# Graph windows and a two-way ConvLSTM scan on one core: another row order, an earlier start of the scan, fc2 and edge products exchanged, GpSimd released by VectorE's last one-hot

## The chip, the cores and the metric

One core of one Trainium2 chip runs the kernel. It has five engines with queues of their own: TensorE (PE, with its weight loads PEld), VectorE (DVE), ScalarE (ACT), GpSimd (POOL) and SyncE (SP), which here issues nearly all DMAs. The metric is device microseconds (us) of one execution, the median of several.

## The reference, cut to what matters

Two layers follow each other, on x of 16 images, 48 channels, 32 x 32.

```
layer 0 (per 8x8 window, 64 nodes, C=48, O=96, K=9)
  y     = affine(conv1x1(x, fc1))                       # 48 -> 48
  idx   = top_k(-dist(normalised nodes), 9)             # per node, in its window
  feat  = [x_i, x_j - x_i] for the 9 neighbours j
  h     = max over j of gelu(affine(feat @ ew + eb))    # 96 channels
  x1    = affine(conv1x1(h, fc2)) + x                   # 96 -> 48
layer 1 (ConvLSTM scans over the 32 rows of x1, forward and backward)
  step  : gates = conv3 over width of [x1 row, h] + b   # 4 x 48 channels
          c = sigmoid(f)*c + sigmoid(i)*tanh(g);  h = sigmoid(o)*tanh(c)
  y     = w_proj @ [h_forward, h_backward]
  out   = relu(batchnorm(y)) + x1                       # statistics over all positions
```

## The kernel before, in words

**Stages.** First fc1, the node norms and their splits into parts (to some 78 us). Then the windows stage: 32 *turns*, each for one group g of 8 windows (a strip of 8 image rows and two images, 512 nodes), till some 368 us. Then the scan stage: 32 steps with two directions d, each step one row forward and one backward, with the projection in its second half. Last the statistics, relu and the final sum.

**Every engine has a program of its own**, written out in `build` and tied to the others by semaphores (`wait_ge`, `then_inc`). Nothing reorders it: an instruction that waits holds all behind it on its engine. `turns` writes a first turn pair, a loop over most, and the last three pairs unrolled. `nth(j, b, k)` is the group k turns ahead of the present one.

**One turn g on TensorE** (its `turn`): `gather` 0, `edges_rest` and `own` of g+1, `gather` 1, `fc2` of g-1, `gather` 2, `edges` of g+2, `gather` 3, `keys` of g+4. A `gather` (L607) is 8 matmuls into one half of `pz`: one-hot columns pick the neighbours' products. `edges` (L568, L570) makes the products of nodes with edge weights, from `y_hl`, which a DMA brings from `y_d`. `own` (L592) makes the node's own product into `p_out`; `fc2` (L615) writes other partitions of the same bank and so waits for the self-gelu of g+1 that reads it.

**ScalarE**: gelu 0, `ab_low`, self-gelu of g+1, gelu 1, `x1_high` of g-2, gelu 2, `fc2_out` of g-1, gelu 3, `ab_high` of g+2. **VectorE**: the maximum over neighbours of each gelu tile (`maxima` 0 to 3, L1153), with `one_hot` halves of g+1 (L1138) and `topk` of g+3 (L1121, L1129) between them, then `self_max` (L1145), both writing `hmax`. **GpSimd**: `x1_low` of g-2 and `residual` of g-1 (L1046, L1041; "x1 operations" below), released once a turn by VectorE's last `topk` operation. **SyncE**: in a turn the `y_hl` load of g+3, the residual input, `idx` of g+3 out, x1 of g-2 out, keys of g+5 in, `idx` spread to 64 partitions (`ib`).

**fp32r heads and rests.** Values are split into a rounded head and the rest. The scan's weights `wl_raw` are loaded in 11 DMAs in turn 26, scaled on GpSimd in turns 27 and 28, and split on VectorE behind the last turn: `w_xh` (head), `wl_head`, `wl_rest` and `w_e`; four DMAs then move parts of `wl_rest` into rows of `w_xh`. x1 lies in `xh`: its rest in partitions 0 to 47, its head in 64 to 111; `load_twins` and `load_third` copy head channels into the free partitions 48 to 63, 112 to 127, and into `ht`.

**The scan.** TensorE: `x_part` (L679, x1 row with `w_xh`), `h_part` (L693, edge products of h with `w_e`; L700, `ht` with `w_xh`). ScalarE: tanh of the gates (L880, L886), copies of h (L901, L895), tanh of the cell (L890). VectorE: four cell operations (L1232, L1238, L1241, L1248) and the rest of h (L1222). In steps 26 to 29 SyncE also loads x1 rows for the end into `x1r`, in front of its `ht` thirds.

## Time and profile before

| | us |
|---|---|
| median of 3 runs | 699.86 (699.62 to 704.42) |
| the profiled execution | 700.8, span 699.0 |
| TensorE / VectorE / ScalarE / GpSimd busy | 596.8 / 545.6 / 467.0 / 121.2 |
| chain that ended last, by engine | PE 46%, ACT 17%, DVE 13%, issue 13%, DMA 6% |

Busy shares are averages over all stages. In a timeline row stand start and duration in us, the engine and line, what it writes from what, how many were merged, and in brackets the idle time in front with what ended it. A gap is worth something only where other work waits behind it.

### The profile page before, as it was taken

The numbers are of one execution on the slowest core, as the hardware profiler recorded it, in microseconds if no ns is written. First come the engines' busy times: TensorE is split into PE (matmuls) and PEld (weight loads), VectorE is DVE, ScalarE is ACT, GpSimd is POOL, SyncE is SP. The second block draws the span as 40 slices with busy tenths as digits, with TensorE's granted clock in tenths as the row PEclk, the third lists the DMA queues.
The fourth block names the chain that finished last, engine by engine and source line by source line (L and its number), as shares of the span: only waits on it lengthen the run. The fifth ranks groups of instructions, "written<-read, shape, count | busy, mean of one in ns | idle before, by whom it ended". The sixth has DMA issues, their size and how long they took to land.

```text
span 699.0 us, 12676 instructions
## 1 busy us (share of the span) xinstructions
PE 596.8 (85%) x3384; PEld 341.3 (49%) x3384; DVE 545.6 (78%) x1030; ACT 467.0 (67%) x669; POOL 121.2 (17%) x106
## 2 busy tenths in 40 slices
PE   5966799999999999996864988888888999989880
PEld 1212555555555555553532555555555555555540
DVE  2668789999999999994874777777777778777775
ACT  3722468888888888884781666666666666766565
POOL 2620102222222222233537000000000000000000
PEclk9967699999999999997996999999999999999995
DMA  9847575566556656668512211111111222147525
GB/s 224 257 133 198 158 152 130 125 133 130 129 129 129 129 129 129 129 152 166 106 26 37 50 44 46 46 46 44 47 31 31 75 71 74 53 114 153 137 59 180
DMA packets 99228, 75.61 MB, mean 108 GB/s; under 512 B 51988, under 2 KB 81174, under 8 KB 98870
## 3 DMA queue, kind: packets, MB, share of 16 engines
q1 hardware_dynamic: 98438, 71.68, 44.0%
q10 hardware_dynamic: 768, 3.67, 2.1%
q8 instruction: 10, 0.16, 0.1%
q14 instruction: 12, 0.10, 0.1%
HBM read 48.56 MB, written 22.15 MB: 101 GB/s over the span
## 4 chain that ended last, share of the span: by engine, by line
PE 46%; ACT 17%; DVE 13%; issue 13%; DMA 6%; SPq 3%; ACTq 1%; DVEq 0%
PE pz L607 14%; PE pz L700 7%; PE pz L693 6%; PE p_out L615 4%; ACT he L895 3%; ACT tgo L886 3%; DMA y_d<-y 3%; ACT gel L826 3%; PE p_edge L568 3%; PE p_keys L555 2%; PE pz L679 2%; ACT selfg L820 2%; ACT tif L880 2%; PE p_edge L570 2%; DMA y_hl<-y_d 2%
## 5 line engine op out<-in xcount | busy, mean ns | idle before, releaser
L1153 DVE TENSOR_REDUCE hmax<-gel 96x128 f32<-96x1024 f32 x128 | 154.1, 1205 | 33.3 <-ACT gel L826 32.4
L826 ACT ACTIVATE gel<-pz 96x1024 f32<-96x1024 f32 x128 | 130.7, 1023 | 58.2 <-PE pz L607 56.7
L679 PE MATMUL pz<-xh,w_xh 128*112 (+1 forms) x384 | 102.9, 404 | 7.7 <-issue 7.7
L700 PE MATMUL pz<-ht,w_xh 128*112 128x512 f32 x384 | 107.2, 415 | 2.4 <-DMA ht<-xh 2.4
L890 ACT ACTIVATE tc<-c 48x512 f32<-48x512 f32 x64 | 40.2, 627 | 68.1 <-DVE c L1241 68.1
L679 PEld LDWEIGHTS pz<-xh,w_xh 128*112 128x112 f32 x384 | 68.2, 178 | 33.2 <-issue 9.4
L700 PEld LDWEIGHTS pz<-ht,w_xh 128*112 128x112 f32 x384 | 62.3, 175 | 43.1 <-issue 23.6
L1248 DVE SCALAR_TENSOR_TENSOR h<-tgo,tc 48x512 f32<-48x512 f32 x64 | 43.9, 687 | 49.4 <-ACT tc L890 49.4
L693 PE MATMUL pz<-ht,w_e 48*112 48x512 f32 x192 | 60.5, 422 | 23.5 <-ACT he L895 23.5
L1046 POOL TENSOR_TENSOR xh<-kl,xh 48x512 f32 (+1 forms) x32 | 38.6, 1208 | 175.1 <-DVE idx L1129 90.0
L1232 DVE SCALAR_TENSOR_TENSOR cu<-tif,c 48x512 f32<-48x512 f32 x64 | 44.1, 689 | 23.5 <-ACT tif L880 21.9
L607 PE MATMUL pz<-onehot,ab_hi 64*96 64x512 f32 x256 | 61.2, 474 | 1.2 <-ACT gel L826 1.0
L693 PE MATMUL pz<-he,w_e 48*112 48x512 f32 x192 | 61.8, 428 | 0.0
L880 ACT ACTIVATE tif<-pz 112x512 f32<-112x512 f32 x64 | 38.3, 598 | 34.8 <-PE pz L700 34.0
L693 PEld LDWEIGHTS pz<-ht,w_e 48*112 48x112 f32 x192 | 28.5, 174 | 58.4 <-issue 56.0
L607 PE MATMUL pz<-ident,ab_hi 64*96 64x512 f32 x256 | 51.6, 398 | 0.0
L607 PE MATMUL pz<-ident,ab_lo 64*96 64x512 f32 x256 | 51.5, 398 | 0.0
L607 PE MATMUL pz<-onehot,ab_lo 64*96 64x512 f32 x256 | 51.4, 397 | 0.0
L1041 POOL TENSOR_TENSOR kl<-side,kr 48x512 f32<-48x512 f32 x32 | 44.5, 1390 | 24.7 <-ACT side L833 18.0
L1138 DVE TENSOR_SCALAR onehot<-ib,jcol_sb 128x1024 fp32r<-128x1024 uint16 x64 | 48.4, 757 | 0.0
L615 PE MATMUL p_out<-hmax,w_sb 96*48 96x512 f32 x64 | 34.0, 613 | 15.0 <-ACT selfg L820 9.4
L1222 DVE TENSOR_TENSOR ht<-h,ht 48x512 fp32r<-48x512 f32 x62 | 42.5, 686 | 4.7 <-ACT ht L901 4.1
(124 smaller groups left out, 1023.3 us busy)
## 6 DMA issues: line engine op xcount, KB each, us to landing
ib<-idx_d SPq DMA_DIRECT2D x64, 256.0 KB, 4.4
y_d<-y SPq DMA_DIRECT2D x32, 192.0 KB, 3.2
y_hl<-y_d SPq DMA_DIRECT2D x32, 192.0 KB, 4.3
hist_d<-h SPq DMA_DIRECT2D x62, 96.0 KB, 1.9
hp<-hist_d SPq DMA_DIRECT2D x30, 192.0 KB, 2.6
kr<-xn_d SPq DMA_DIRECT2D x32, 98.0 KB
xn_d<-x_in SPq DMA_DIRECT2D x32, 96.0 KB, 2.1
kl<-xn_d SPq DMA_DIRECT2D x32, 96.0 KB
```

The costliest lines, as they stand in the source:

```text
L607: mm = pe.matmul(pz[0:O, 2 * (t % 2) + s, :], part[rows, b, t, which], moving[rows], start=(n == 0), stop=(n == 3))
L615: pe.matmul(p_out[HALF:TOP, :], w2_sb[:, :], hmax[:, b], start=True, stop=True) \
L679: pe.matmul(pz[0:TOP, 2 * d + m, :], w_xh[:, 0, d, m, t], rhs, start=(t == 0), stop=False)
L693: pe.matmul(pz[0:TOP, 2 * d + m, :], w_e[rows, d, m, t], moving(src, rows, t), start=False, stop=False)
L700: mm = pe.matmul(pz[0:TOP, 2 * d + m, :], w_xh[:, 1, d, m, t], moving(ht, slice(0, P), t), start=False, stop=(t == TAPS - 1))
L826: act.activation(gel[:, t % 2], pz[0:O, 2 * (t % 2):2 * (t % 2) + 2, :], ACT.Gelu) \
L880: act.activation(tif[0:TOP, d], pz[0:TOP, 2 * d, :], ACT.Tanh).then_inc(S["tanh_if"], 1)
L1041: pool.tensor_tensor(kl[HALF:TOP, b], side[HALF:TOP], kr[HALF:TOP, b], ALU.add) \
L1138: dve.tensor_scalar(onehot[:, b, 2 * half:2 * half + 2], ib[:, b, 2 * half:2 * half + 2], jcol_sb[:, 0:1], None, ALU.is_equal).then_inc(S[ ...
L1153: dve.tensor_reduce(dst, gel[:, t % 2].rearrange("p w (r c k) -> p w r c k", r=WS, k=KN), AX_X, ALU.max).then_inc(S["maxed"], 1)
L1232: dve.scalar_tensor_tensor(cu[HALF:TOP, d], tif[HALF:TOP, d], 1.0, c2[HALF:TOP, d], ALU.add, ALU.mult)
L1248: dve.scalar_tensor_tensor(h2[0:C, d], tgo[HALF:TOP, d], 1.0, tc[HALF:TOP, d], ALU.add, ALU.mult) \
```

## The change

The diff has these parts.

- **Row order.** `place(g)` maps the groups' strips of 8 rows to the order 0, 3, 2, 1, so that the first 16 groups give both ends of the image. Host data are read in that order; `store_x1`, `slots` and `load_xres` use it.
- **Exchanged products.** On TensorE `edges` of g+2 stands behind gather 1 and `fc2` of g-1 behind gather 2.
- **Spread weight split.** The 11 loads are issued in turn 24, the scaling is in turns 26 and 27, and VectorE's split lies in pieces in turns 29 to 31, where it has no `topk`: three heads, two masked products that write `w_xh` (head times a column `rests` of 0 or -1, plus raw), and `w_e`. The column is filled by a memset and four tiny DMAs; the four DMAs of rests are gone.
- **Immediate scan.** Twins are copied in turns 28 and 29. TensorE starts the scan when gelu 2 of the last turn has freed its half of `pz` and both masked products are there; step 0 leaves out the six edge products of each direction (h is 0). fc2, its output and the x1 operations of the last group lie within steps 0 and 1, SyncE's constants behind step 1.
- **GpSimd** waits for `onehots` (the second half of g+1) where it waited for `topk_done` of g+3.
- **x1r.** GpSimd's memset of unused partitions is gone; one DMA more for every four rows fills them.
- One turn pair more is unrolled.

```diff
-            wl_head = a("wl_head", [P, 2, 2, TAPS, TOP], F32R)
-            wl_rest = a("wl_rest", [P, 2, 2, 2, TAPS, TOP], F32R)
+            wl_head = a("wl_head", [P, 3, 2, 2, TAPS, TOP], F32R)
         x1r = sb("x1r", [P, H // 2, B * W], F32)
         w_xh = sb("w_xh", [P, 2, 2, 2, TAPS, TOP], F32R)
...
             for b in range(2):
                 turn(0, b)
-            with engine.Fori(1, GROUPS // 2 - 3) as j:
+            with engine.Fori(1, GROUPS // 2 - 4) as j:
                 for b in range(2):
                     turn(j, b)
-            for j in range(GROUPS // 2 - 3, GROUPS // 2):
+            for j in range(GROUPS // 2 - 4, GROUPS // 2):
                 for b in range(2):
                     turn(j, b)
...
-            wr, p = g // PAIRS, g % PAIRS
+            wr, p = place(g)
             return xh[first:first + C, reg(wr * WS, 0, WS), 0:(W + 1) * B] \
                 .rearrange("c r (h n) -> c h r n", h=2)[:, :, :, reg(p * (W + 1), 1, W)]
+
+        def place(g):
+
+            return g // PAIRS * 3 % WROWS, g % PAIRS
         def by_row(t):
...
-
-            def move_scan_weights():
-
-                sp.wait_ge(S["wl_split"], 3)
-                for k, first, n in ((0, C, HALF - C), (0, TOP, P - TOP), (1, C + 1, 1), (1, TOP, P - TOP)):
-                    sp.dma_start(w_xh[first:first + n, k].bitcast(F32), wl_rest[first:first + n, k].bitcast(F32)) \
-                        .then_inc(S["wl_moved"], 16)
+                sp.wait_ge(S["rests_set"], 1)
+                for k, first, n in ((0, C, HALF - C), (0, TOP, P - TOP), (1, C + 1, HALF - C - 1), (1, TOP, P - TOP)):
+                    sp.dma_start(rests[first:first + n, k:k + 1], ones_sel[0:n, 0, 0:1],
+                                 allow_slow_non_contiguous=True).then_inc(S["rests_here"], 16)
             def load_twins(s, d, b):
...
                     .then_inc(S[f"x_third{d}"], 16)
             def turn(j, b):
-                if isinstance(j, int) and nth(j, b, 0)[0] == GROUPS - 6:
+                if isinstance(j, int) and nth(j, b, 0)[0] == GROUPS - 8:
                     load_scan_weights()
-                if isinstance(j, int) and nth(j, b, 0)[0] == GROUPS - 2:
+                if isinstance(j, int) and nth(j, b, 0)[0] in (GROUPS - 4, GROUPS - 3):
+                    d = nth(j, b, 0)[0] - (GROUPS - 4)
+                    sp.wait_ge(S["x1_hi"], 2 * PAIRS)
+                    sp.wait_ge(S["pads_set"], 9)
                     for s in range(2):
-                        load_twins(s, 0, s)
-                    sp.wait_ge(S["pads_set"], 9)
-                    load_third(0, 0)
+                        load_twins(s, d, s)
+                    load_third(0, d)
                 for k, stage in ((3, load_y), (0, load_xres), (3, store_idx), (-2, store_x1), (5, load_keys),
                                  (3, spread_idx)):
...
             turns(sp, turn)
             store_x1(GROUPS - 2, 0, GROUPS // 2 - 1)
-            move_scan_weights()
-            sp.wait_ge(S["x1_hi"], GROUPS)
-            for s in range(2):
-                load_twins(s, 1, s)
-            load_third(0, 1)
-            store_x1(GROUPS - 1, 1, GROUPS // 2 - 1)
...
                     load_h(s - 1, 1 - b)
             step(0, 0)
-            with sp.Fori(0, H // 4 - 2) as j:
+            store_x1(GROUPS - 1, 1, GROUPS // 2 - 1)
+            step(1, 1)
+            for b in range(2):
+                sp.wait_ge(S[f"x1_stored{b}"], 32 * (GROUPS // 2))
+            sp.wait_ge(S["x1_split"], GROUPS)
+            sp.dma_start(wp_sb[:], wp).then_inc(S["consts2"], 16)
+            sp.dma_start(wp_low[:], wp[C:O]).then_inc(S["consts2"], 16)
+            sp.dma_start(gb_sb[:], gb).then_inc(S["consts2"], 16)
+            sp.dma_start(comb_sb[:], comb).then_inc(S["consts2"], 16)
+            with sp.Fori(1, H // 4 - 1) as j:
                 for b in range(2):
-                    s = j * 2 + (1 + b)
+                    s = j * 2 + b
                     for d in range(2):
                         load_third(s + 1, d)
-                        load_twins(s + 2, d, 1 - b)
+                        load_twins(s + 2, d, b)
                         store_h(s, d)
-            for s in range(13, 18):
+            for s in range(14, 18):
                 step(s, s % 2)
             with sp.Fori(0, H // 4 - 4) as j:
                 for b in range(2):
                     step(j * 2 + (18 + b), b)
-            sp.wait_ge(S["x1r_pads"], 1)
+            sp.wait_ge(S["wl_split"], 3)
             with sp.Fori(0, 2) as j:
                 for b in range(2):
                     i = j * 8 + 4 * b
                     sp.dma_start(x1r[0:C, reg(i, 0, 4)], x1_d[reg(i, H // 2, 4)].rearrange("r c b w -> c r (b w)")) \
+                        .then_inc(S["x1r_loaded"], 16)
+                    sp.dma_start(x1r[C:HALF, reg(i, 0, 4)],
+                                 x1_d[reg(i, H // 2, 4), 0:HALF - C].rearrange("r c b w -> c r (b w)")) \
                         .then_inc(S["x1r_loaded"], 16)
                     for k in range(4):
...
                 on(1, edges_rest)
                 on(1, own)
                 gather(g, 1, b)
+                on(2, edges)
+                gather(g, 2, b)
                 on(-1, fc2)
-                gather(g, 2, b)
-                on(2, edges)
                 gather(g, 3, b)
                 on(4, keys)
...
                 if later(s, H // 2 + 2):
                     project(s - (H // 2 + 2), b, (s - (H // 2 + 2)) // 2)
-            pe.wait_ge(S["gelus"], 4 * GROUPS)
-            pe.wait_ge(S["wl_split"], 4)
-            pe.wait_ge(S["wl_moved"], 64)
+            pe.wait_ge(S["x1_split"], 2 * PAIRS)
             pe.wait_ge(S["zeros_set"], 2)
+            pe.wait_ge(S["wl_split"], 2)
+            pe.wait_ge(S["gelus"], 4 * GROUPS - 1)
             x_part(0, 0, 0, 0)
             h_part(0, 0)
-            pe.wait_ge(S["x1_split"], GROUPS)
+            pe.wait_ge(S["gelus"], 4 * GROUPS)
             x_part(0, 1, 0, 0)
             h_part(0, 1)
             x_part(1, 0, 1, 0)
+            fc2(GROUPS - 1, 1, GROUPS // 2 - 1)
+            pe.wait_ge(S["wl_split"], 3)
             with pe.Fori(0, H // 4 - 1) as j:
                 for b in range(2):
...
                     if more:
                         h_edge(*prev)
+                    if isinstance(s, int) and s == 0 and d == 1:
+                        fc2_out(GROUPS - 1, 1, GROUPS // 2 - 1)
                     tanh_cell(s, d)
                     if d == 0:
                         tanh_i_f(s, 1)
                     elif not isinstance(s, int) or s + 1 < H:
                         tanh_i_f(s + 1, 0)
+                    if isinstance(s, int) and s == 1 and d == 0:
+                        x1_high(GROUPS - 1, 1, GROUPS // 2 - 1)
                     if d == 0 and projects:
                         keep(s - (H // 2 + 3), 1 - b)
             tanh_i_f(0, 0)
             step(0, 0)
-            with act.Fori(0, H // 4) as j:
+            step(1, 1)
+            step(2, 0)
+            with act.Fori(1, H // 4) as j:
                 for b in range(2):
...
                     pool.tensor_scalar(ap, ap, 0.5, 1.0, ALU.mult, ALU.mult).then_inc(S["wl_scaled"], 1)
                     pool.wait_ge(S["wl_scaled"], n)
-                pool.wait_ge(S["x1_sum"], GROUPS - 5 + part)
+                pool.wait_ge(S["x1_sum"], GROUPS - 6 + part)
                 if part == 0:
                     pool.wait_ge(S["wl_loaded"], 11 * 16)
+                    pool.wait_ge(S["rests_here"], 4 * 16)
+                    pool.tensor_scalar(rests[:], rests[:], -1.0, 1.0, ALU.mult, ALU.mult).then_inc(S["rests_set"], 1)
+                    pool.wait_ge(S["rests_set"], 2)
...
                                    ALU.subtract).then_inc(S["x1_split"], 1)
             def turn(j, b):
-                if exists(nth(j, b, 3)[0]):
-                    pool.wait_ge(S["topk_done"], nth(j, b, 4)[0])
+                if exists(nth(j, b, 1)[0]):
+                    pool.wait_ge(S["onehots"], nth(j, b, 2)[0] * 2)
                 for k, stage in ((-2, x1_low), (-1, residual)):
                     if exists(nth(j, b, k)[0]):
...
                 dve.tensor_reduce(dst, gel[:, t % 2].rearrange("p w (r c k) -> p w r c k", r=WS, k=KN),
                                   AX_X, ALU.max).then_inc(S["maxed"], 1)
-            def scan_weights():
-
-                dve.wait_ge(S["wl_scaled"], 9)
-                dve.tensor_copy(w_xh[:], wl_raw[:, 0:2]).then_inc(S["wl_split"], 1)
-                dve.tensor_copy(wl_head[:], wl_raw[:, 2]).then_inc(S["wl_split"], 1)
-                dve.wait_ge(S["wl_split"], 1)
-                dve.tensor_tensor(wl_rest[:], wl_raw[:, 0:2], w_xh[:].bitcast(F32), ALU.subtract) \
-                    .then_inc(S["wl_split"], 1)
-                dve.wait_ge(S["wl_split"], 2)
-                dve.tensor_tensor(w_e[:], wl_raw[:, 2], wl_head[:].bitcast(F32), ALU.subtract).then_inc(S["wl_split"], 1)
+            def scan_weights(g, part):
+
+                def head(k):
+                    dve.tensor_copy(wl_head[:, k], wl_raw[:, k]).then_inc(S["wl_heads"], 1)
+
+                def masked(k):
+                    dve.wait_ge(S["wl_heads"], k + 1)
+                    dve.scalar_tensor_tensor(w_xh[:, k], wl_head[:, k].bitcast(F32), rests[:, k:k + 1], wl_raw[:, k],
+                                             ALU.mult, ALU.add).then_inc(S["wl_split"], 1)
+
+                if g == GROUPS - 3:
+                    if part == 0:
+                        dve.wait_ge(S["wl_scaled"], 9)
+                    head(part)
+                elif part == 0:
+                    masked(g - (GROUPS - 2))
+                elif g == GROUPS - 2:
+                    head(2)
+                else:
+                    dve.wait_ge(S["wl_heads"], 3)
+                    dve.tensor_tensor(w_e[:], wl_raw[:, 2], wl_head[:, 2].bitcast(F32), ALU.subtract) \
+                        .then_inc(S["wl_split"], 1)
             def turn(j, b):
                 now = nth(j, b, 0)
                 maxima(*now, 0)
                 on(1, one_hot, 0)
                 on(3, topk, 0)
+                if not exists(nth(j, b, 3)[0]):
+                    scan_weights(now[0], 0)
                 maxima(*now, 1)
                 on(1, one_hot, 1)
                 on(3, topk, 1)
+                if not exists(nth(j, b, 3)[0]):
+                    scan_weights(now[0], 1)
                 maxima(*now, 2)
                 maxima(*now, 3)
                 self_max(*now)
-                if not exists(nth(j, b, 1)[0]):
-                    scan_weights()
             for c in range(10):
```

TensorE, the loop's turn, before: from gather 1 to the edge products (`p_out<-hmax` is fc2, `p_edge<-we_hi,y_hl` edges).

```order
L607 MATMUL pz<-onehot,ab_hi 96x512 [waits gelus,onehots]
L607 MATMUL pz<-onehot,ab_hi 96x512
L607 MATMUL pz<-onehot,ab_lo 96x512 x2
L607 MATMUL pz<-ident,ab_hi 96x512 x2
L607 MATMUL pz<-ident,ab_lo 96x512 x2
L615 MATMUL p_out<-hmax,w_sb 48x512 [waits self_gel,self_maxed]
L607 MATMUL pz<-onehot,ab_hi 96x512 [waits gelus,onehots]
L607 MATMUL pz<-onehot,ab_hi 96x512
L607 MATMUL pz<-onehot,ab_lo 96x512 x2
L607 MATMUL pz<-ident,ab_hi 96x512 x2
L607 MATMUL pz<-ident,ab_lo 96x512 x2
L568 MATMUL p_edge<-we_hi,y_hl 128x192 [waits ab_low,y_loaded0]
```

Now the edge products come directly behind gather 1:

```order
L607 MATMUL pz<-onehot,ab_hi 96x512 [waits gelus,onehots]
L607 MATMUL pz<-onehot,ab_hi 96x512
L607 MATMUL pz<-onehot,ab_lo 96x512 x2
L607 MATMUL pz<-ident,ab_hi 96x512 x2
L607 MATMUL pz<-ident,ab_lo 96x512 x2
L568 MATMUL p_edge<-we_hi,y_hl 128x192 [waits ab_low,y_loaded0]
L570 MATMUL p_edge<-we_lo,y_hl 128x192
```

and fc2 behind gather 2, ahead of gather 3:

```order
L570 MATMUL p_edge<-we_lo,y_hl 128x192
L607 MATMUL pz<-onehot,ab_hi 96x512 [waits gelus,onehots]
L607 MATMUL pz<-onehot,ab_hi 96x512
L607 MATMUL pz<-onehot,ab_lo 96x512 x2
L607 MATMUL pz<-ident,ab_hi 96x512 x2
L607 MATMUL pz<-ident,ab_lo 96x512 x2
L615 MATMUL p_out<-hmax,w_sb 48x512 [waits self_gel,self_maxed]
L607 MATMUL pz<-onehot,ab_hi 96x512 [waits gelus,onehots]
```

The wait for `y_loaded` has moved ahead of gather 2 and fc2, the wait for `self_gel` behind it.

VectorE at the end of the windows stage, before (L1232 is the scan's first cell operation):

```order
L1145 TENSOR_TENSOR hmax<-hmax,selfg 96x512
L1153 TENSOR_REDUCE hmax<-gel 96x2x8x8 x4
L1145 TENSOR_TENSOR hmax<-hmax,selfg 96x512
L1159 CAST w_xh<-wl_raw 128x2688
L1160 CAST wl_head<-wl_raw 128x1344
L1162 TENSOR_TENSOR wl_rest<-wl_raw,w_xh 128x2688
L1165 TENSOR_TENSOR w_e<-wl_raw,wl_head 128x1344
L1232 SCALAR_TENSOR_TENSOR cu<-tif,c 48x512
```

and with the change, from the `self_max` of turn 30:

```order
L1151 TENSOR_TENSOR hmax<-hmax,selfg 96x512
L1159 TENSOR_REDUCE hmax<-gel 96x2x8x8
L1169 SCALAR_TENSOR_TENSOR w_xh<-wl_head,rests,wl_raw 128x1344
L1159 TENSOR_REDUCE hmax<-gel 96x2x8x8
L1182 TENSOR_TENSOR w_e<-wl_raw,wl_head 128x1344
L1159 TENSOR_REDUCE hmax<-gel 96x2x8x8 x2
L1151 TENSOR_TENSOR hmax<-hmax,selfg 96x512
L1252 SCALAR_TENSOR_TENSOR cu<-tif,c 48x512
```

The split has moved from between the last `self_max` and the first cell operation to places between maxima.

TensorE at the start of the scan, before:

```order
L615 MATMUL p_out<-hmax,w_sb 48x512 [waits self_gel,self_maxed]
L679 MATMUL pz<-xh,w_xh 112x512 [waits zeros_set,wl_moved,x_twin00,wl_split,gelus]
L679 MATMUL pz<-xh,w_xh 112x512 x5
L693 MATMUL pz<-ht,w_e 112x512
...
L700 MATMUL pz<-ht,w_xh 112x512 [waits x_third0]
L700 MATMUL pz<-ht,w_xh 112x512 x5
L679 MATMUL pz<-xh,w_xh 112x512 [waits x_twin10,x1_split]
```

and with the change:

```order
L678 MATMUL pz<-xh,w_xh 112x512 [waits gelus,wl_split,x_twin00,zeros_set,x1_split]
L678 MATMUL pz<-xh,w_xh 112x512 x5
L699 MATMUL pz<-ht,w_xh 112x512 [waits x_third0]
L699 MATMUL pz<-ht,w_xh 112x512 x5
L678 MATMUL pz<-xh,w_xh 112x512 [waits x_twin10,gelus]
L678 MATMUL pz<-xh,w_xh 112x512 x5
L699 MATMUL pz<-ht,w_xh 112x512 [waits x_third1]
...
L678 MATMUL pz<-xh,w_xh 112x512 [waits x_twin01,tanh_if]
...
L615 MATMUL p_out<-hmax,w_sb 48x512 [waits self_gel,self_maxed]
```

The edge products (L693) and the waits for `wl_moved` are gone, and fc2 of the last group has moved behind three x parts.

## Rows read from the trace of the kernel before

**Rows 1.** The page's first line.
```profile
span 699.0 us, 12676 instructions
```

**Rows 2.** Stretches: length, busy us (instructions) by engine, granted clock share, DMA share, GB/s.
```profile
101.71:317.20 215.49, 207.48 (x1626) 122.47 (x1626) 200.48 (x477) 181.93 (x226) 61.77 (x50) 1.00 0.62 133
322.00:331.00 9.00, 5.37 (x35) 3.98 (x37) 0.42 (x2) 1.36 (x2) 3.89 (x7) 0.60 0.70 154
```

**Rows 3.** Waits from 100 to 340 us: total, times, longest.
```profile
PE p_out L615 <- ACT selfg L820: 8.1, 26, 0.4
```

**Rows 4.** Timeline of TensorE, one turn: start, duration, what, idle before it.
```profile
213.88 1.03 PE L615 MATMUL p_out<-hmax,w_sb 96*48 96x512 f32 x2 [0.29 <-ACT selfg L820]
214.84 0.47 PE L607 MATMUL pz<-onehot,ab_hi 64*96 64x512 f32 x2
...
215.94 0.36 PE L568 MATMUL p_edge<-we_hi,y_hl 97*128 97x192 f32 x1
...
218.01 0.28 PE L551 MATMUL p_keys<-mask_r,mask_l 64*128 64x256 bf16 x1
```

**Rows 5.** Timeline of VectorE, the same turns.
```profile
212.01 0.78 DVE L1145 TENSOR_TENSOR hmax<-hmax,selfg 96x512 f32<-96x512 f32 x1
...
215.04 1.20 DVE L1153 TENSOR_REDUCE hmax<-gel 96x128 f32<-96x1024 f32 x1
216.16 0.74 DVE L1138 TENSOR_SCALAR onehot<-ib,jcol_sb 128x1024 fp32r<-128x1024 uint16 x1
...
217.49 0.22 DVE L1129 FIND_INDEX8 idx<-val,p_keys 128x8 uint16<-128x64 f32 x1
...
219.26 1.22 DVE L1153 TENSOR_REDUCE hmax<-gel 96x128 f32<-96x1024 f32 x1 [0.44 <-ACT gel L826]
220.59 0.69 DVE L1145 TENSOR_TENSOR hmax<-hmax,selfg 96x512 f32<-96x512 f32 x1
```

**Rows 6.** Timeline of GpSimd, a turn and the second scaling part.
```profile
210.97 1.28 POOL L1041 TENSOR_TENSOR kl<-side,kr 48x512 f32<-48x512 f32 x1
...
342.09 4.82 POOL L1022 TENSOR_SCALAR wl_raw<-wl_raw 48x1344 f32<-48x1344 f32 x3
```

**Rows 7.** Timeline of SyncE's DMA issues in turns 25 and 26.
```profile
300.16 0.47 SPq L290 DMA_DIRECT2D y_hl<-y_d  x1
...
309.16 4.92 SPq L388 DMA_DIRECT2D wl_raw<-wl  x11
```

**Rows 8.** Timeline of TensorE, the late edge products of turn 27.
```profile
325.63 0.53 PE L568 MATMUL p_edge<-we_hi,y_hl 97*128 97x192 f32 x1 [6.29 <-DMA y_hl<-y_d]
```

**Rows 9.** Timeline of VectorE, from turn 28 to the scan's first cell.
```profile
340.89 1.22 DVE L1153 TENSOR_REDUCE hmax<-gel 96x128 f32<-96x1024 f32 x1 [0.46 <-ACT gel L826]
342.21 1.73 DVE L1145 TENSOR_TENSOR hmax<-hmax,selfg 96x512 f32<-96x512 f32 x1
...
355.58 1.33 DVE L1138 TENSOR_SCALAR onehot<-ib,jcol_sb 128x1024 fp32r<-128x1024 uint16 x1
...
368.27 1.54 DVE L1159 CAST w_xh<-wl_raw 128x2688 fp32r<-128x2688 f32 x1
...
373.38 1.54 DVE L1165 TENSOR_TENSOR w_e<-wl_raw,wl_head 128x1344 fp32r<-128x1344 f32 x1
383.83 0.69 DVE L1232 SCALAR_TENSOR_TENSOR cu<-tif,c 48x512 f32<-48x512 f32 x1 [8.91 <-ACT tif L880]
```

**Rows 10.** Timeline of TensorE, scan step 0 and the start of step 1.
```profile
378.07 2.87 PE L679 MATMUL pz<-xh,w_xh 128*112 128x512 f32 x6 [7.73 <-issue]
...
389.62 0.46 PE L693 MATMUL pz<-ht,w_e 48*112 48x512 f32 x1 [0.45 <-ACT he L895]
```

**Rows 11.** The page's groups: busy us, mean ns, idle before them and releaser.
```profile
L700 PE MATMUL pz<-ht,w_xh 128*112 128x512 f32 x384 | 107.2, 415 | 2.4 <-DMA ht<-xh 2.4
...
L880 ACT ACTIVATE tif<-pz 112x512 f32<-112x512 f32 x64 | 38.3, 598 | 34.8 <-PE pz L700 34.0
```

**Rows 12.** The page's DMA issues: KB each, us to landing.
```profile
y_hl<-y_d SPq DMA_DIRECT2D x32, 192.0 KB, 4.3
```

46 lines of the change are left out of this document (18 added, 28 removed).

## Prediction

> **What bounds the kernel now.** The page gives the span [rows 1]. The granted-clock and busy view by stretches then shows two long stages, a windows stage and a scan stage, with a gap between. In the windows stage 25 turns take 215.49 us, 8.62 us each; VectorE is busy for 200.48 of it, 8.02 a turn, and TensorE's clock is at its upper level, 2.4 GHz [rows 2]. Neither is saturated, so I looked for what the one waits for that ends last. The waits view names it: TensorE stood 8.1 us in 26 pieces before the second layer's product (fc2, L615) until ScalarE had made the self-gelu [rows 3]. The timeline of one turn shows its order: fc2 is in front of the third gather and the edge products [rows 4], so everything behind it starts late. VectorE idles 0.44 us once in a turn [rows 5].
>
> One turn is different: SyncE issues 11 loads of scan weights in a burst, the `y_hl` load queued behind it arrives only as TensorE's edge product can start at 325.63, 6.29 us late, and the clock falls to its lower level (mean 0.60 in that stretch), so that the first edge product takes 0.53 us in place of 0.36 [rows 2, 4, 7, 8].
>
> Then the change of stages: from VectorE's fourth maximum of turn 28 at 340.89 to the first weight product of scan step 1 at 389.62 are 48.7 us [rows 9, 10]. The last piece of it is pure serial work: weight split on VectorE from 368.27, its second part by DMA, scan matmuls from 378.07 on, first cell operation at 383.83.
>
> **Exchanged products.** TensorE's second gather is now followed by edge products and the third gather, 2.1 us of work (a gather is 1.10, from 214.84 to 215.94; edges and a gather are 2.07, to 218.01) [rows 4], and only then by fc2 (0.96). The self-gelu was 0.3 us late, so this covers it. The wait is 8.1/26 = 0.31 us a turn. What is late next: VectorE has 0.44 us of slack, its last search of a turn ends at 217.71 and the keys product that waits for it starts at 218.01 [rows 4, 5], so some 0.1 us stays before that becomes the wait. I take the full 0.31 for 26 turns: **-8.1 us** (ends: 0, and 0.44 x 26 = -11.4, where VectorE would be full).
>
> **The burst.** It moves from turn 26 to turn 24, with four tiny DMAs more. `y_hl` should still arrive about 16.5 us after the first load is issued, at 309.16 before [rows 7, 8]. But edges now stand in front of a gather and of fc2, so these, 1.10 + 0.96 us, which were done before the stall, are done behind it, at the slow clock (0.53/0.36, some 1.5 times): 3.1 us. The shorter turns also reach the wait some 0.5 us earlier in their schedule; against that, the turn after the stall then runs at the high clock where it was half slow. **+3.0 us** (0 to +7).
>
> **GpSimd's release.** Its two x1 operations start behind the last one-hot and no longer behind the last search, about 0.8 us earlier. Before, the second ran from 210.97 to 212.25 and touched VectorE's `hmax` operation at 212.01 [rows 5, 6]; in a turn 0.3 us shorter it would overlap more, with the new release it does not. What lies beside it now are searches and a maximum, and maxima lay beside GpSimd already. I cost it at nothing (ends -1 and +2 us in all); its cover is the slack between the last one-hot and `hmax`. Row order adds register work on GpSimd, ScalarE and SyncE, hidden in their idle time.
>
> **Scaling of the weights on GpSimd** moves from turns 27 and 28 to 26 and 27. Its first part lay in the stall; the second collided with `hmax`, 1.73 us in place of 0.69 [rows 5, 6, 9]. Now both meet a busy VectorE: **+1.0 us** (0 to +3).
>
> **Spread split and immediate scan.** The 16 first window groups now are the image rows that both scan directions begin with, so step 0 needs only the weights, free PSUM and VectorE. With the waits on the last x1, on the DMA of the rests, and on `w_e` gone, VectorE's own queue decides. Counted from 340.89, by the spacings in [rows 5, 9]: a maximum is 1.12 us (215.04 to 216.16), or 1.33 where `hmax` waits for its completion (219.26 to 220.59); `hmax` is 0.69, a one-hot 0.74 less the same overlap of 0.08. The rest of turn 28 is 1.33 + 0.69 = 2.0. Turns 29 to 31 hold nine maxima at 1.12 (10.1), three at 1.33 (4.0), three `hmax` (2.1), four one-hots (2.6), three heads at half of the 1.54 that the double-sized cast took (2.3), and two masked products and `w_e` at 1.54 each (4.6; the masked ones have the size of `w_e`). Together 27.7 us, without a gap: end at 368.6, where the first cell operation can start, against 383.83: **-15.2 us**. TensorE is ready before that: behind the second masked product VectorE still has three maxima, `w_e` and `hmax` to do, 5.8 us, so that product ends near 362.8. The 12 matmuls of step 0, forward, take 5.7 us by the slow row at 378.07 (2.87 us for six), half of it at the fast clock, and two tanh at 0.6 follow [rows 10, 11]: the input of `cv` is there between 366.9 and 369.7, against a need at 369.3. The six edge products that step 0 no longer computes are hidden then.
>
> Off that term goes contention. Seven x1 operations of GpSimd fall into this tail, where VectorE is the path. Rows show a one-hot of 1.33 us instead of 0.74 and a `hmax` of 1.73 instead of 0.69 [rows 5, 9]; I take two of the smaller kind, and some, **+1.5 us** (0 to +6).
>
> The switch from gelu to tanh on ScalarE lay in idle time. The Trainium skill (ScalarE: Activation LUTs, "What ACT_TABLE_LOAD costs") gives 2.66 us for a switch of table sets; by that, step 0's tanh would end about when VectorE is free, and the sum would be some 0.4 us higher. No row shows such a load by itself.
>
> The last fc2, its output, residual and x1 operations slip into steps 0 and 1, in idle time of TensorE and ScalarE, but beside cell operations on VectorE: **+0.5 us** (0 to +3). GpSimd's memset of `x1r` behind the last x1 goes; nothing waited for it before the loads of step 26.
>
> **The x1r load** gets a DMA more for every four rows in steps 26 to 29. TensorE waited 2.4 us for `ht` thirds in the whole trace [rows 11], in two pieces, both in these steps, behind these loads. One issue more is 0.45 us for SyncE (4.92 for eleven, [rows 7]), and about 0.5 us of transfer: **+2.0 us** over four batches, the two that had waited in full and the others in part (0 to +5).
>
> **Sum:** -8.1 + 3.0 + 1.0 - 15.2 + 1.5 + 0.5 + 2.0 = -15.3 us. The profiled execution took 700.8 us around its span of 699.0, so it should become 685.5; against the median of 699.86 that is **684.6 us**. With the ends of the single terms the likeliest case lies between 679 and 691. About 1% (7 us) is what can be told from no change.
>
> **Rivals.**
> 1. *The turn does not shrink* (12%). VectorE's search, 0.3 us before the keys product, or the one-hots become the wait as soon as fc2 goes. For: 8.02 of 8.62 us are busy. Against: it still idles 0.44. The -8.1 falls away: 692.7.
> 2. *Contention takes the tail* (12%). VectorE's two-input operations of the tail (two masked products, `w_e`, three `hmax`) each meet a GpSimd operation and wait it out whole: six at 1.28 [rows 6] are 7.7 us in place of 1.5, which makes 690.8. For: `hmax` lost 1.04 to one scaling operation. Against: GpSimd is idle most of a turn and the pairs need not meet. The Trainium skill (SBUF — State Buffer, "Who interferes with whom") states this rule, an exclusive lock in which the later one blocks fully; the rows agree in kind, with 0.6 and 1.0 us.
> 3. *A second stall behind the burst* (8%). Behind it now come two more turns with keys loads, where one had none. If the next `y_hl` or keys are late as well, another 6.3 us and some 2 us for the slow clock: 692.9. Against: the queue had drained one turn later.
> 4. *Slower: `y_hl` is late in every turn* (5%). Edges stand 2.1 us earlier in the turn, in a turn 0.3 us shorter, and a gather now queues behind them. The load of 300.16 [rows 7] is issued 4.6 us behind a keys product (218.01 plus nine turns is 295.6), and its edges come two turns less 2.1 us behind that same product, 15.2: 10.6 us for a load that lands in 4.3 [rows 4, 12]. After the change 7.9 us are left. It decides from a landing of 7.9 us on; at 9.0 each of 25 turns loses 1.1: +27.5, which makes 712. Against: the only slow one in the trace is behind the burst.
>
> That step 0 does not start early would need the order of the program not to hold; it does hold in all engines' queues, so I leave it 1%.
>
> **How the numbers follow.** My forecast has 62%, the rivals 12, 12, 8 and 5, the rest 1. Under it, 684.6 with 679 to 691; rivals 1 to 3 end at 690 to 693, some at the border of 1%, which is 692.9. So faster 0.84, same 0.11, slower 0.05. The range reaches over rivals 1 and 2 above and, below, over burst and loads costing nothing: 678 to 693.5.
>
> **What would show it.** In the profile after: turns of about 8.3 us (fc2 to fc2) and no wait before fc2; if 8.6 stays, rival 1, and VectorE has no idle piece. A stall before the edge products of some 9 us two turns earlier, with a gather and fc2 at the slow clock behind it. VectorE without a gap from turn 29 to its first cell operation, and this about 28 us behind the fourth maximum of turn 28; durations over 1.5 us in `hmax` or the masked products are the contention. Two to four waits for `ht` thirds of 1 to 2 us near the end. The prediction is wrong if ScalarE or TensorE, not VectorE, releases step 0, or if `y_hl` waits appear in more than one turn.

## The result, and the profile after

The changed kernel takes 682.74 us (median of 4, 680.25 to 684.85) against 700.11 (699.62 to 704.42) for the kernel before on the same chip: a ratio of 0.9737, 95% interval 0.9687 to 0.9788. That is 17.4 us less. The forecast was 684.6, and the size is right. One term is given to the wrong cause, and four others are off by about 1 us each. The profiled execution took 682.53 us, 18.3 less in its span than [rows 1].

The page's first line:
```profile
span 680.7 us, 12599 instructions
```
Stretches as in [rows 2]: 22 turns, the stretch of the late edge products, and the tail.
```profile
100.37:283.15 182.78, 182.49 (x1433) 107.72 (x1431) 176.38 (x419) 160.13 (x198) 54.23 (x44) 1.00 0.56 134
294.00:312.00 18.00, 13.24 (x81) 7.93 (x81) 5.89 (x10) 7.34 (x9) 1.28 (x1) 0.68 0.66 148
332.69:360.73 28.04, 24.17 (x140) 14.41 (x141) 27.59 (x28) 21.40 (x27) 13.35 (x8) 1.00 0.27 61
```
A turn is 182.78/22 = 8.31 us, where it was 8.62 [rows 2]. TensorE is now busy in 99.8% of it: 182.49 of 182.78, against 207.48 of 215.49 before. VectorE is busy 8.02 us a turn, as before. The waits view from 95 to 320 us no longer has the row of [rows 3]:
```profile
PE p_edge L568 <- DMA y_hl<-y_d: 9.4, 1, 9.4
PEld p_keys L551 <- DVE idx L1135: 8.0, 22, 0.4
```
In this window TensorE waits once, behind the burst; the second row is a weight load that waits beside running matmuls and costs nothing. Ahead of the window, in the first turn, there is a second wait for `y_hl` that the kernel before doesn't have:
```profile
82.29 0.36 PE L568 MATMUL p_edge<-we_hi,y_hl 97*128 97x192 f32 x1 [0.75 <-DMA y_hl<-y_d]
```

VectorE in one turn, and GpSimd beside it:
```profile
193.66 1.20 DVE L1159 TENSOR_REDUCE hmax<-gel 96x128 f32<-96x1024 f32 x1
195.04 1.22 DVE L1159 TENSOR_REDUCE hmax<-gel 96x128 f32<-96x1024 f32 x1 [0.19 <-ACT gel L829]
196.37 0.69 DVE L1151 TENSOR_TENSOR hmax<-hmax,selfg 96x512 f32<-96x512 f32 x1
```
```profile
193.50 1.18 POOL L1057 TENSOR_TENSOR xh<-kl,xh 48x512 f32 x1 [5.54 <-DVE onehot L1144]
194.76 1.28 POOL L1052 TENSOR_TENSOR kl<-side,kr 48x512 f32<-48x512 f32 x1
```
GpSimd's residual (L1052) ends at 196.04, 0.33 us before `hmax` (L1151) starts. That `hmax` is the only VectorE operation of a turn with two inputs from SBUF; keep it in mind.

The burst: SyncE's queue, then TensorE (they answer to [rows 7, 8]).
```profile
281.85 6.06 SPq L392 DMA_DIRECT2D wl_raw<-wl  x11
287.95 2.18 SPq L395 DMA_DIRECT2D rests<-ones_sel  x4
290.18 0.42 SPq L294 DMA_DIRECT2D y_hl<-y_d  x1
```
```profile
298.75 0.53 PE L568 MATMUL p_edge<-we_hi,y_hl 97*128 97x192 f32 x1 [9.42 <-DMA y_hl<-y_d]
...
302.66 1.94 PE L615 MATMUL p_out<-hmax,w_sb 96*48 96x512 f32 x2
```
The edge products start 16.9 us behind the first load (forecast: 16.5), and fc2 behind them takes 1.94 us at the lower level of the clock, where it is 1.06 in other turns.

VectorE from turn 28 to the first cell operation (answers to [rows 9]), and GpSimd at its end:
```profile
331.57 2.32 DVE L1159 TENSOR_REDUCE hmax<-gel 96x128 f32<-96x1024 f32 x2
...
336.40 0.85 DVE L1165 CAST wl_head<-wl_raw 128x1344 fp32r<-128x1344 f32 x1
...
352.83 1.60 DVE L1169 SCALAR_TENSOR_TENSOR w_xh<-wl_head,rests,wl_raw 128x1344 fp32r<-128x1344 f32 x1
...
355.49 1.54 DVE L1182 TENSOR_TENSOR w_e<-wl_raw,wl_head 128x1344 fp32r<-128x1344 f32 x1
...
359.39 1.31 DVE L1151 TENSOR_TENSOR hmax<-hmax,selfg 96x512 f32<-96x512 f32 x1
360.73 0.69 DVE L1252 SCALAR_TENSOR_TENSOR cu<-tif,c 48x512 f32<-48x512 f32 x1
```
```profile
352.83 2.65 POOL L1057 TENSOR_TENSOR xh<-kl,xh 48x512 fp32r<-48x512 f32 x1 [1.70 <-ACT xh L842]
355.56 2.63 POOL L1052 TENSOR_TENSOR kl<-side,kr 48x512 f32<-48x512 f32 x1
358.94 1.21 POOL L1057 TENSOR_TENSOR xh<-kl,xh 48x512 fp32r<-48x512 f32 x1 [0.75 <-ACT xh L842]
```
The fourth maximum of turn 28 is the second of the two at 331.57, and starts 1.12 us later, at 332.69 (an operation begins 1.12 behind the maximum ahead of it). From there VectorE shows no idle piece up to `cu` at 360.73: 28.04 us, where it was 42.94 (340.89 to 383.83, [rows 9]). ScalarE's last copy of x1 and the first tanh of step 0 in the same stretch:
```profile
358.22 0.64 ACT L842 ACTIVATE xh<-kl 48x512 fp32r<-48x512 f32 x1 [1.54 <-POOL kl L1052]
358.89 0.60 ACT L881 ACTIVATE tif<-pz 112x512 f32<-112x512 f32 x1
```

TensorE near the end, the waits for thirds of `ht` (two, 2.4 us, in [rows 11]):
```profile
607.65 1.69 PE L699 MATMUL pz<-ht,w_xh 128*112 128x512 f32 x6 [2.23 <-DMA ht<-xh]
...
617.61 1.68 PE L699 MATMUL pz<-ht,w_xh 128*112 128x512 f32 x6 [0.45 <-DMA ht<-xh]
...
628.87 2.22 PE L699 MATMUL pz<-ht,w_xh 128*112 128x512 f32 x6 [1.75 <-DMA ht<-xh]
```

### The profile page after: what moved, and what is told of

Read it like the earlier page. It is cut to its first block, busy times and chain, and to the rows that moved or that the text cites. A ratio compares the mean times of both kernels' runs of the same rounds, so it can differ in the third digit from the quotient of the medians.

```text
span 680.7 us, 12599 instructions
## 1 busy us (share of the span) xinstructions
PE 589.5 (87%) x3372; PEld 338.4 (50%) x3372; DVE 543.9 (80%) x1032; ACT 467.3 (69%) x669; POOL 115.8 (17%) x107
## 4 chain that ended last, share of the span: by engine, by line
PE 51%; DVE 16%; ACT 12%; issue 9%; DMA 6%; SPq 4%; ACTq 1%; DVEq 0%
PE pz L607 16%; PE pz L699 8%; PE pz L693 7%; PE p_out L615 4%; ACT he L896 4%; DVE hmax L1159 3%; ACT tgo L887 3%; DMA y_d<-y 3%; PE p_keys L555 2%; PE p_edge L568 2%; PE pz L678 2%; PE p_edge L578 2%; ACT tif L881 2%; PE p_edge L570 2%; DVE onehot L1144 1%
## 5 line engine op out<-in xcount | busy, mean ns | idle before, releaser
L699 PE MATMUL pz<-ht,w_xh 128*112 128x512 f32 x384 | 108.8, 419 | 4.4 <-DMA ht<-xh 4.4
L693 PE MATMUL pz<-ht,w_e 48*112 48x512 f32 x186 | 58.2, 419 | 25.9 <-ACT he L896 25.9
L1057 POOL TENSOR_TENSOR xh<-kl,xh 48x512 f32 (+1 forms) x32 | 40.5, 1264 | 167.1 <-DVE onehot L1144 157.9
L693 PE MATMUL pz<-he,w_e 48*112 48x512 f32 x186 | 59.5, 426 | 0.0
L693 PEld LDWEIGHTS pz<-ht,w_e 48*112 48x112 f32 x186 | 27.3, 171 | 60.2 <-issue 57.9
L1052 POOL TENSOR_TENSOR kl<-side,kr 48x512 f32<-48x512 f32 x32 | 42.3, 1323 | 30.5 <-ACT side L836 28.3
L1261 DVE SCALAR_TENSOR_TENSOR c<-cu,cv 48x512 f32<-48x512 f32 x64 | 44.1, 690 | 2.2
```

The costliest lines, as they stand in the source:

```text
L693: pe.matmul(pz[0:TOP, 2 * d + m, :], w_e[rows, d, m, t], moving(src, rows, t), start=False, stop=False)
L699: mm = pe.matmul(pz[0:TOP, 2 * d + m, :], w_xh[:, 1, d, m, t], moving(ht, slice(0, P), t), start=False, stop=(t == TAPS - 1))
L1261: dve.scalar_tensor_tensor(c2[HALF:TOP, d], cu[HALF:TOP, d], 0.5, cv[HALF:TOP, d], ALU.mult, ALU.add) \
```

## The experiments

Each kernel is the changed one with one edit, and those with "version" in their expectation build on each other. The work up to the keys product of the first turn is nearly the same in all of them, and yet this product comes at 84.47 to 87.52 us (85.92 in the changed kernel). So two columns leave that start out: **A** is the time from this product to the first cell update `c`, **B** from there to the last `c`. "Turn" is the mean over the 23 turns from the next keys product on, waits for `y_hl` in it included. The versions whose weight loads are spread also unroll more turn pairs, 6 (loads spread) or 10 (the others). The kernel before took 699.86 to 701.50 us on the chips of these runs.

| kernel | median us | ratio to before, 95% | turn | A | B |
|---|---|---|---|---|---|
| before | 700.11 | | 8.63 | 297.68 | 290.02 |
| changed | 682.74 | 0.9687 to 0.9788 | 8.31 | 276.23 | 294.27 |
| products back | 692.34 | 0.9813 to 0.9893 | 8.62 | 285.01 | 296.09 |
| GpSimd behind the search | 691.36 | 0.9856 to 0.9916 | 8.64 | 283.66 | 294.78 |
| neither of the two | 690.46 | 0.9770 to 0.9908 | 8.64 | 285.03 | 294.10 |
| x1 first | 691.70 | 0.9790 to 0.9910 | 8.30 | 286.38 | 292.80 |
| split behind | 687.74 | 0.9762 to 0.9858 | 8.30 | 282.65 | 293.21 |
| heads on ScalarE | 683.02 | 0.9680 to 0.9781 | 8.31 | 277.26 | 297.57 |
| memset of x1r | 678.05 | 0.9631 to 0.9718 | 8.31 | 276.73 | 291.43 |
| loads spread | 673.97 | 0.9596 to 0.9652 | 8.41 | 267.31 | 294.80 |
| single loads, memset | 668.56 | 0.9492 to 0.9625 | 8.32 | 263.98 | 292.77 |
| + scaling behind hmax | 669.81 | 0.9485 to 0.9602 | 8.36 | 264.82 | 293.86 |
| + heads on GpSimd | 667.80 | 0.9474 to 0.9594 | 8.34 | 263.78 | 291.91 |
| + load behind y_hl | 666.21 | 0.9454 to 0.9541 | 8.27 | 262.06 | 291.61 |

### Which edit shortened the turn

**Products back**, and **GpSimd behind the search**:
```diff
-                on(2, edges)
-                gather(g, 2, b)
                 on(-1, fc2)
+                gather(g, 2, b)
+                on(2, edges)
                 gather(g, 3, b)
```
```diff
-                if exists(nth(j, b, 1)[0]):
+                if exists(nth(j, b, 3)[0]):
+                    pool.wait_ge(S["topk_done"], nth(j, b, 4)[0])
+                elif exists(nth(j, b, 1)[0]):
                     pool.wait_ge(S["onehots"], nth(j, b, 2)[0] * 2)
```


> The changed kernel with one part undone: on TensorE the fc2 product of the group before last and the edge products of the group after next stand again in the order of before (fc2 ahead, edge products behind). Theory (the exchange is worth 0.3 us a turn): between two fc2 products 8.62 us again in place of 8.31, 22 turns and the two of the start, so about 7.4 to 8 us longer up to the burst of weight loads; at the burst fc2 no longer stands behind an edge product that waits for the residual, which gives 1 to 3 back. Total 688 to 690 us against 682.7. Rival (the 0.3 us a turn came from the earlier release of GpSimd or from another wait that the new order of x1_low and the residual took off, not from the exchange): the turn stays at 8.31, total 680 to 683.

> The changed kernel with one part undone: GpSimd waits again for the end of the whole search of VectorE in a turn, not for the last one-hot of the turn, before it makes x1_low and the residual. Theory (the release is worth nothing, since the residual is done long before the edge products that read it): turn 8.31 as in the changed kernel, total 682.7 within -1 to +2. Rival (the release carries part of the 0.3 us a turn, since the residual now lies beside the GELU product's maximum and the edge products wait for it): 0.3 to 0.7 us a turn more, 28 turns, total 690 to 700, and a wait of TensorE for GpSimd ahead of the edge products that the changed kernel does not have.

Each edit taken back alone gives the whole 0.3 us back: 8.62 and 8.64. For the first that is what the theory said (its 692.3 us are 2 above the theory's total, since B is 1.8 longer, in the last five steps where loads wait), for the second it is the rival's size (691.4 us, not 682.7), but with the wait in another place: not TensorE for GpSimd, but VectorE's own operation becomes longer. Then both together (the two edits above in one kernel):

> The changed kernel with both the order of the products and the release of GpSimd as before. Each of them undone alone gave turns of 8.63 and 8.65 us in place of 8.31. Theory (two bounds lie one behind the other, TensorE's wait for the self-gelu and VectorE's hmax behind the residual of GpSimd, and each edit takes off one, so that only both pay): turns of 8.62 to 8.66, total 689 to 692, no slower than either alone. Rival (the two are independent costs of 0.3 us each that add up): turns of 8.95, total near 700.

8.64 again, 690.46 us: the rival (8.95) is out. The costs are not added but stand one behind the other. The waits views from 100 to 280 us, first of the kernel with the products back, then of the one with GpSimd behind the search:
```profile
PE p_out L615 <- ACT selfg L823: 6.6, 21, 0.4
```
```profile
PEld p_keys L551 <- DVE idx L1137: 14.2, 21, 0.9
ACT gel L829 <- DVE hmax L1161: 8.3, 10, 0.9
```
and the turn of that second kernel on VectorE and GpSimd:
```profile
197.29 2.32 DVE L1161 TENSOR_REDUCE hmax<-gel 96x128 f32<-96x1024 f32 x2
199.71 1.32 DVE L1153 TENSOR_TENSOR hmax<-hmax,selfg 96x512 f32<-96x512 f32 x1
200.96 1.20 DVE L1161 TENSOR_REDUCE hmax<-gel 96x128 f32<-96x1024 f32 x1
```
```profile
197.95 1.19 POOL L1057 TENSOR_TENSOR xh<-kl,xh 48x512 f32 x1 [6.04 <-DVE idx L1137]
199.21 1.27 POOL L1052 TENSOR_TENSOR kl<-side,kr 48x512 f32<-48x512 f32 x1
```
The residual is still running when `hmax` is due, and `hmax` takes 1.32 in place of 0.69 us. Over 21 turns (grouped by line, three kernels: GpSimd behind the search, neither, changed):
```profile
L1153 DVE TENSOR_TENSOR hmax<-hmax,selfg 96x512 f32<-96x512 f32 x21 | 28.8, 1373 | 2.3
```
```profile
L1153 DVE TENSOR_TENSOR hmax<-hmax,selfg 96x512 f32<-96x512 f32 x21 | 21.2, 1009 | 2.3
```
```profile
L1151 DVE TENSOR_TENSOR hmax<-hmax,selfg 96x512 f32<-96x512 f32 x22 | 15.1, 689 | 2.4
```
VectorE's 8.02 us of a turn and 1.37 - 0.69 = 0.68 more are 8.70, a little over its turn of 8.64: VectorE is full. The stretches view of that kernel has it busy for 177.61 of 180 us:
```profile
100.00:280.00 180.00, 174.83 (x1357) 102.17 (x1356) 177.61 (x394) 152.68 (x188) 51.93 (x42) 1.00 0.55 129
```
In the kernel with neither edit the overlap is there too (1.01), but VectorE still has slack, and TensorE's wait for the self-gelu is back (7.0 us in 21 pieces): it sets 8.64.

### The tail

**x1 first** moves fc2, its output and x1 of the last group ahead of step 0 on TensorE and ScalarE, with a wait for all x1; **split behind** takes VectorE's split out of the turns:
```diff
             turns(pe, turn)
+            fc2(GROUPS - 1, 1, GROUPS // 2 - 1)
+            pe.wait_ge(S["x1_hi"], GROUPS)
```
```diff
             turns(dve, turn)
+            scan_weights()
```


> The changed kernel with the immediate start of the scan undone and the rest kept: TensorE and ScalarE finish fc2, its output and x1 of the last group before step 0, and step 0 waits for the last x1. Theory: fc2 1.0, its output 0.8, residual 1.3, x1_high 0.6, step 0's products 4.2 and tanh 0.6 all stand behind VectorE's last maximum, about 8.5 us in all, and the 1.3 us that the late fc2 costs in steps 0 to 2 come back: first cell operation 36 to 37 us behind the fourth maximum of turn 28 (28.0 in the changed kernel), total 689.5 to 690.5. Rival (step 0 was released by the split of the weights and not by the row order, so that the last x1 lies beside it): 1 to 3 us, total 683 to 685.5.

> The changed kernel with the split of the scan's weights (three heads, two masked products, w_e: 6.9 us on VectorE) in one piece behind the last turn, in place of one or two of its operations in each of the turns 29 to 31. Theory (spreading pays only by letting TensorE and ScalarE do step 0 beside VectorE's last operations; VectorE's own sum is the same): turns end 6.9 us earlier on VectorE, the second masked product 4.6 us behind that, step 0's products and tanh 4.7 us behind that, so the first cell operation comes 30 to 31 us behind the fourth maximum of turn 28, where it is 28.0; total 684.5 to 686. Rival (in the turns the split lies in VectorE's idle time, so that putting it behind costs all of it): 34.9 us, total 689.6.

From the fourth maximum of turn 28 to the first cell operation the changed kernel has 28.04 us. The columns of VectorE's timeline, x1 first and then split behind:
```profile
361.10 1.25 DVE L1150 TENSOR_TENSOR hmax<-hmax,selfg 96x512 f32<-96x512 f32 x1
372.05 0.69 DVE L1251 SCALAR_TENSOR_TENSOR cu<-tif,c 48x512 f32<-48x512 f32 x1 [9.71 <-ACT tif L884]
```
```profile
341.58 1.22 DVE L1159 TENSOR_REDUCE hmax<-gel 96x128 f32<-96x1024 f32 x1 [0.87 <-ACT gel L829]
...
367.88 0.69 DVE L1245 SCALAR_TENSOR_TENSOR cu<-tif,c 48x512 f32<-48x512 f32 x1 [2.67 <-ACT tif L881]
```
Their fourth maxima start at 334.41 and 333.74. So x1 first has 37.64, 9.6 us more, of which 1.2 come back in steps 0 to 2 (B is 1.47 shorter): the theory, 0.6 us above its range; the rival's 1 to 3 us are out. The excess is mostly TensorE's clock behind its wait for `hmax` (0.52 from 358 to 372 us): fc2 took 1.94 us where the theory had 1.0. Step 0's products were at the lower clock too (2.90 us for the first six, 1.66 in the changed kernel), but from their start at 367.21 to the tanh at 371.43 they took the 4.2 us of the theory.
```profile
362.40 1.94 PE L615 MATMUL p_out<-hmax,w_sb 96*48 96x512 f32 x2 [6.32 <-DVE hmax L1150]
```
Split behind has 34.14, 6.1 us more, near its rival's 34.9, and 687.74 us lies between the two forecasts. Both had a part: VectorE idled 2.4 us in turns 29 to 31, waiting for gelus (0.87 of it above), which the split had filled; and behind the second masked product stood step 0's products and tanh, at the lower clock, with 4.8 us, the theory's 4.7. The two parts, 9.6 + 6.1 = 15.7, are near what the tail gained (14.9); that they add up isn't shown, since each was undone with the other in place.

**Heads on ScalarE**:
```diff
+                def head(k):
+                    act.wait_ge(S["wl_scaled"], 9)
+                    act.activation(wl_head[:, k], wl_raw[:, k], ACT.Copy).then_inc(S["wl_heads"], 1)
...
-                def head(k):
-                    dve.tensor_copy(wl_head[:, k], wl_raw[:, k]).then_inc(S["wl_heads"], 1)
```


> The changed kernel with the three head casts of the scan's weights (0.77 us each on VectorE) moved to ScalarE, in turns 29 and 30; VectorE keeps the two masked products and w_e. Theory (VectorE's own queue is the path from turn 28 to the first cell operation): that operation comes 28.0 - 2.3 = 25.7 us behind the fourth maximum of turn 28, total 680.4 against 682.7. Rival (TensorE, released by the last GELU products and the second masked product, is as late as VectorE): the tanh of step 0 ends 0.4 us before VectorE is free in the changed kernel, so the first cell operation moves by 0.4 to 1 us alone, and waits for ScalarE's tif; total 681.7 to 682.3.

Neither: the tail became longer, 29.18 us. ScalarE and then VectorE:
```profile
345.56 1.33 ACT L851 ACTIVATE wl_head<-wl_raw 128x1344 fp32r<-128x1344 f32 x1
```
```profile
337.99 1.22 DVE L1170 TENSOR_REDUCE hmax<-gel 96x128 f32<-96x1024 f32 x1 [0.98 <-ACT gel L829]
...
339.84 1.22 DVE L1170 TENSOR_REDUCE hmax<-gel 96x128 f32<-96x1024 f32 x1 [0.63 <-ACT gel L829]
```
A head costs ScalarE 1.33 us, VectorE 0.77 (a row of 0.85, but the next operation starts 0.08 before its end). VectorE saves 2.3 and waits 3.1 for gelus in turns 29 and 30, where ScalarE is now busy for 18.68 of 19.55 us (15.21 of 18.40 in the changed kernel). VectorE is full in the changed kernel's tail, but ScalarE has too little room there for three more operations ahead of its gelus.

### The end, and the burst

**Memset of x1r**: the extra DMA for each four rows goes, and GpSimd's memset is back.
```diff
-                    sp.dma_start(x1r[C:HALF, reg(i, 0, 4)],
-                                 x1_d[reg(i, H // 2, 4), 0:HALF - C].rearrange("r c b w -> c r (b w)")) \
-                        .then_inc(S["x1r_loaded"], 16)
...
+            pool.memset(x1r[32:HALF], 0.0).then_inc(S["x1r_pads"], 1)
```


> The changed kernel without the extra transfer for rows 48 to 63 of the reversed copy of x1: those rows are set to zero once by GpSimd behind the last x1, as in the kernel before, and no output depends on them. Theory (that transfer, one more in each of the eight loads of the last steps on SyncE's queue, makes the last rows of the scan late): cells from (27,0) to the end come 2.5 to 3 us earlier, total 679.5 to 680.5 against 682.7. Rival (the late rows hang on the row transfers as a whole, and the one more is nothing): less than 0.5 us, total 682.3 to 682.7.

B is 291.43, 2.84 us shorter: the theory holds. The median is 4.7 less, where the theory had 2.2 to 3.2; the rest lies in the other stages, in the profiled executions 1.4 of it in the start. The changed kernel and the seven others with the extra DMA differ by up to 2.1 us among each other from step 25 to step 31, but all four later versions without it are, with this one, 1.8 to 2.9 us shorter there than the changed kernel. The three waits of TensorE for `ht` are 2.13 in all, where they were 4.43 (two of the three):
```profile
605.70 1.67 PE L696 MATMUL pz<-ht,w_xh 128*112 128x512 f32 x6 [1.07 <-DMA ht<-xh]
...
625.76 1.68 PE L696 MATMUL pz<-ht,w_xh 128*112 128x512 f32 x6 [0.73 <-DMA ht<-xh]
```

**Loads spread** over six turns, then **single loads** over eleven:
```diff
-                if isinstance(j, int) and nth(j, b, 0)[0] == GROUPS - 8:
-                    load_scan_weights()
...
+                if isinstance(j, int) and GROUPS - 12 <= nth(j, b, 0)[0] < GROUPS - 6:
+                    load_scan_weights(nth(j, b, 0)[0] - (GROUPS - 12))
```


> The changed kernel with the eleven loads of the scan's weights and the four of the rests no longer issued in one go at turn 24 on SyncE's queue, but one to three at a time behind the other work of turns 20 to 25. Theory (the burst delays the y_hl loads that the edge products read by one whole wait, 9.42 us of idle TensorE, and what follows at the lower clock): the wait is gone, total 9 to 11 us less, 672 to 674. Rival (the transfers themselves, not their issue in one go, take the time, or the turn after has no room for the scaling): half of it or less, total 677 to 682.

> A version from the experiments: the changed kernel with rows 48 to 63 of x1's reversed copy set to zero once by GpSimd in place of the extra transfer, and the eleven loads of the scan's weights one to a turn in turns 12 to 22, the four of the rests in turn 23. Theory (spread over six turns the loads still left waits of TensorE for y_hl of 2.7 us in all, from two or three loads in one turn; one to a turn leaves none): 2 to 3 us below the sum of the two single experiments (682.7 - 8.8 - 4.7 = 669.2), so 666 to 668. Rival (one large load in a turn delays the y_hl behind it as much as two do): 668.5 to 671, with y_hl waits in several turns.

Spread, the median is 8.8 us less and A 8.9, 673.97 in all: the theory. The waits left (2.7 us) are mostly one:
```profile
282.82 0.36 PE L571 MATMUL p_edge<-we_hi,y_hl 97*128 97x192 f32 x1 [2.11 <-DMA y_hl<-y_d]
```
Single loads leave one of 0.6, and A is 3.3 shorter still. By A that is the theory. The median, 668.56, is just in the rival's range and only 0.6 below the sum of the two single experiments (B gave back 1.3), but what the rival named, waits in several turns, isn't there.

### What the experiments point to

> The version with single loads, and the scaling of the weights by GpSimd cut into three parts in turns 24 to 26 in place of two in turns 26 and 27, each behind VectorE's hmax of its turn. Theory (in the changed kernel the scaling holds hmax up once, 1.68 in place of 0.69 us, and one-hots by 0.2, so behind hmax it costs nothing): 0.8 to 1.5 us less than the version with single loads, no hmax over 0.8 us in turns 24 to 28. Rival (the scaling then meets one-hots and maxima and costs as much there): within 0.3 us of it.

> The version with scaling behind hmax, and the three head casts moved from VectorE to GpSimd, in turns 27 and 28 behind hmax. Theory (VectorE and ScalarE share the tail: without any part of the split VectorE still waited 2.4 us for ScalarE's gelus in turns 29 to 31, so of the 2.3 us of heads about half lies in such waits): first cell operation 1 to 1.5 us earlier against the fourth maximum of turn 28, total 1 to 1.5 us less. Rival (ScalarE is the path of the tail as soon as the heads go, as in the version with the heads on ScalarE): less than 0.4 us.

> The version with the heads on GpSimd, and each single load of the scan's weights issued right behind the y_hl load of its turn in place of right ahead of the next turn's y_hl. Theory (the waits for y_hl that were left, 1.5 us in two pieces, come from the largest loads standing directly ahead of y_hl in SyncE's queue): no wait for y_hl before TensorE's edge products in turns 12 to 28, 1 to 1.5 us less than before, total 666 to 667. Rival (the weight loads take the time of the DMA engines wherever they stand, and delay the keys or the gathers' indices instead): no gain, total 667.5 to 669.

```diff
+                pool.wait_ge(S["self_maxed"], GROUPS - 8 + part + 1)
...
+                for k in ((0, 1) if g == GROUPS - 5 else (2,)):
+                    pool.tensor_copy(wl_head[:, k], wl_raw[:, k]).then_inc(S["wl_heads"], 1)
...
+                    if stage is load_y and isinstance(j, int) and GROUPS - 20 <= nth(j, b, 0)[0] < GROUPS - 8:
+                        load_scan_weights(nth(j, b, 0)[0] - (GROUPS - 20))
```
Scaling behind `hmax`: the operation itself is cured, as the timelines show (single loads, then this one), but the time is 1.2 longer and not 0.8 to 1.5 shorter (669.81 against 668.56, intervals overlap):
```profile
311.86 1.69 DVE L1153 TENSOR_TENSOR hmax<-hmax,selfg 96x512 f32<-96x512 f32 x1
```
```profile
313.87 0.69 DVE L1155 TENSOR_TENSOR hmax<-hmax,selfg 96x512 f32<-96x512 f32 x1
```
Its trace has 1.8 us of `y_hl` waits where that of single loads has 0.6, with the same queue; from the last keys product on it is 0.3 us shorter. Neither theory nor rival, and inconclusive. Heads on GpSimd: the first cell operation comes 27.12 us behind the fourth maximum of turn 28, against 28.12, which is the theory's 1 us; but 0.4 of that is lost ahead of this maximum, and from the last keys product to the first `c` it is 38.33 us against 38.97, so 0.6. With the load moved behind `y_hl` the waits for it from turn 2 on fall from 1.5 us to none and A by 1.7: the theory. This version takes **666.21 us**, 0.9498 of before (0.9454 to 0.9541), below both kernels of this case.

## Why the prediction was right, and where it was not

By its own terms, from the two profiles:

| term | forecast | measured |
|---|---|---|
| start, same code | 0 | -1.65 |
| products and release, 26 turns | -8.1 + 0 | -9.5 |
| burst, scaling | +3.0 + 1.0 | +2.9 |
| tail: split, immediate scan, contention | -15.2 + 1.5 | -14.9 |
| last x1 in steps 0 to 2 | +0.5 | +1.3 |
| x1r load, and the last stretch | +2.0 | +2.95 + 0.55 |
| sum | -15.3 | -18.3 |

How the second column is read: the keys product of the first turn comes at 85.92 against 87.57, that of the next turn gains 1.46 more, the next 23 gain 7.40, and two further turns count 0.62. The fourth maximum of turn 28 comes 8.20 earlier (332.69, 340.89), so 9.5 + 1.65 - 8.2 = 2.9 went to burst and scaling. `cu` is 23.1 earlier, the updates from step 2 on 21.8, the last 18.85. The 1.65 of the start belong to no edit: this product comes anywhere from 84.47 to 87.52 in the kernels of the table above, whose work up to there is nearly the same. That they are part of the 18.3 is chance.

- **Exchanged products: the size is right, the step that names its cause failed.** The size is even nearer than the table says. A turn gains 0.32 us, 8.3 in 26 turns. The other 1.1 lie in one turn, where the kernel before waited 1.30 us for a search and then ran at the lower clock (mean 0.83 from 85 to 95 us; 1.00 in the changed kernel). "I cost it at nothing", of GpSimd's release, was half of the pair: with the exchange alone the turn is 8.64, with the release alone 8.62, with neither 8.64, with both 8.31. The prediction had the mechanism in a sentence (a shorter turn lets the residual overlap `hmax` more, the release prevents it) and gave it no price. Whoever had made only the exchange on that sum would have got nothing. It was readable: VectorE busy for 8.02 us has 0.29 of slack in a turn of 8.31, and an `hmax` held up by half of the residual's 1.28 [rows 6] uses up more. Rival 1 was this case, with the wrong operation as the full engine's load.
- **The burst.** One stall, two turns earlier, with a gather and fc2 at the lower clock: as told. With the exchange taken back the three turns around the stall took 37.34 us, 11.5 over three of its own turns; in the changed kernel 37.63, 12.7 over. So the new order costs 1.2 us at the stall, and 3.0 was too much: with the products back the turn behind the stall took 11.51 us, in the changed kernel 8.32. Rival 3 did not come.
- **The tail.** 28.04 us against 27.7 and 1.5 of contention. The contention fell on the other side: while VectorE was first (the masked product at 352.83, `w_e` at 355.49) GpSimd took 2.65 and 2.63 in place of 1.2 and 1.28, and VectorE's own time was 1.60 and 1.54, as without it. VectorE lost 0.62 once, at the `hmax` of 359.39, where GpSimd was first. That is rival 2's mechanism at a tenth of its price, and it is the rule that the Trainium skill states (SBUF — State Buffer, "Who interferes with whom"): who issues first has the ports, and the other waits. Here the trace agrees for both orders; `hmax` lost 0.62 of the 0.76 us for which GpSimd still ran. The prediction counted two-input operations and one-hots; a head cast held GpSimd up as well. `x1_low` took 1.74 us beside the cast of 338.96, and 1.20 at the same place with the heads on ScalarE.
- **Release of step 0.** `cu` started right behind `hmax`. Its input, the first tanh, was done at 359.49, 1.24 us before: VectorE set it. But that tanh stood behind ScalarE's copy of x1 (L842), which waited 1.54 us for the residual that took 2.63. So the contention on GpSimd stayed off the path by 1.24 us; the prediction looked at VectorE's side alone.
- **The switch from gelu to tanh** costs nothing here, so the prediction's 0.4 us falls away. Its "No row shows such a load by itself" doesn't hold: the traces of both kernels have three rows of a table load, 1.28 us each, ahead of the first root (3.57 in both), of the first gelu and of the last root. Between the last gelu and the first tanh there is none.
```profile
72.47 1.28 ACT L823 ACT_TABLE_LOAD   x1 [14.31 <-PE p_out L593]
```
- **Last x1, +1.3 for +0.5.** Most of it is TensorE's clock. From the first `cu` of step 0 to that of step 2 the changed kernel takes 18.53 us, and behind TensorE's wait of 3.18 us for `he` in step 1 one group of six matmuls took 2.90. The kernel before takes 17.37 and x1 first 17.36. But "neither of the two", which keeps the late fc2 output and x1, takes 17.66: there the wait is 1.56 and the clock stays at its upper level. So the late work itself is worth about 0.3 us. Where the lower level lasts longer, as with single loads, it is 19.74.
- **x1r, +2.95 for +2.0.** The three waits are 4.43 us, 2.0 more than the two before, which is the forecast; the six matmuls behind the last of them took 2.22 in place of 1.68, at the lower clock, which it left out. With the extra DMA gone 2.84 us came back. The "0.5 us of transfer" in the term's working stands in no run by itself.
- **`y_hl` late every turn** (the slower rival): it didn't come. But the prediction called itself wrong if `y_hl` waits appear in more than one turn, and by the letter they do: the first turn has one of 0.75 us, where the edge products now stand earlier. It cost that once, and the turns behind it none.

Open: the 1.65 us of the start; why the version with scaling behind `hmax` had more `y_hl` wait than the same queue before; the 0.55 us of the last stretch, which no term forecast; and how much of the tail's gain needs both its edits, since no run undoes them together.

## What to carry to other kernels

When one engine's wait is taken away and the next engine has less slack than the wait was long, price what the shorter turn pushes together on that next engine: here two edits were worth 0.3 us a turn together and nothing apart. A burst of prefetches in an in-order queue can cost its whole length to the first urgent load behind it (8.3 us of issue, a wait of 9.4); with one load a turn, issued right behind the urgent one, no wait for it was left. And an operation moved off the fullest engine pays only by the slack of the engine that takes it.

## What the runs showed of the hardware

- Between a VectorE operation with two fp32 inputs from SBUF and a two-input GpSimd operation, the later waits for nearly all that is left of the earlier: `hmax` 0.69 became 1.25 to 1.43, GpSimd's 1.28 became 2.63. Two operations one behind the other on VectorE held one residual twice (4.81 us in the kernel before, beside `wl_rest` and `w_e`). Maxima (one input) beside the same operations kept 1.20 us, but a one-input head cast held GpSimd up too (1.74 in place of 1.20).
- One table set served gelu and tanh on ScalarE: no ACT_TABLE_LOAD (1.28 us) stands between the last gelu and the first tanh in the traces of the kernels before and changed; each has three, ahead of the first root, of the first gelu and of the last root.
- The same head cast of 128x1344 took VectorE 0.85 us, ScalarE 1.33, GpSimd 1.32 to 1.80.
- After a wait of TensorE of 9 us its work ran at the lower of its clock levels (mean 0.68 in the 18 us around it) for 6.7 us (298.75 to 305.4): fc2 took 1.94 in place of 1.06.
